# Two of eight value taps as ScalarE products that GpSimd adds, in the wavelet-attention and binary-conv kernel

## The reference

```python
x = x + L0(group_norm(x))      # attention over channels
x = x + L1(group_norm(x))      # two binary 3x3 convolutions with batch norms
```

```python
kv = depthwise3x3(einsum('oc,bchw->bohw', qkv_w, x));  k, v = split(kv)
q  = inverse_dwt(depthwise3x3(dwt(x)))                 # a wavelet transform there and back
attn = softmax(normalised(q) @ normalised(k).T * temperature)   # 16x16 a head and image
out  = proj_w @ (attn @ v)
```

## Time and profile before

| | us |
|---|---|
| median of three runs | 1533.03 |
| lowest, highest | 1522.18, 1548.53 |
| the profiled execution | 1536.24 |
| its span | 1534.7 |
| its stretch from 224 to 1006 us, nearly all of `block_grams` | 782 |

### The profile page before, as it was taken

The page is one execution under the profiler, slowest core; times in us unless marked ns, Lnnn a source line. Parts: engine busy times, 40 slices in busy tenths (PEclk is TensorE's granted clock), DMA queues, the critical chain, the costliest instruction groups (busy, mean ns, idle before and its releaser), DMA issues. The chain is left out here.

```text
span 1534.7 us, 35991 instructions
## 1 busy us (share of the span) xinstructions
PE 1222.0 (80%) x12628; PEld 975.4 (64%) x12628; DVE 1140.8 (74%) x1567; ACT 790.9 (52%) x1382; POOL 492.9 (32%) x268
## 2 busy tenths in 40 slices
PE   1797837789898889898988889863699999799910
PEld 0454537779898889897988889851355555455500
DVE  7626938999989899998999999924776673253384
ACT  0475745556555656565655657511134425666473
POOL 1486912344453292542613736311100000000000
PEclk9999958798989899898998999975899999899965
DMA  9975763434343443334343434116877622000059
GB/s 330 365 293 219 305 151 81 116 82 116 83 119 82 121 116 93 107 95 116 90 117 83 119 92 117 60 34 238 288 278 246 204 70 103 1 0 1 0 230 401
DMA packets 147827, 221.12 MB, mean 144 GB/s; under 512 B 115528, under 2 KB 116692, under 8 KB 144096
## 3 DMA queue, kind: packets, MB, share of 16 engines
q1 hardware_dynamic: 137888, 166.41, 34.8%
q0 software_dynamic: 5184, 33.03, 5.8%
q10 hardware_dynamic: 4608, 19.67, 3.2%
HBM read 131.84 MB, written 87.20 MB: 143 GB/s over the span
## 5 line engine op out<-in xcount | busy, mean ns | idle before, releaser
L844 DVE SCALAR_TENSOR_TENSOR b_vacc<-b_vin,b_vtaps,b_vacc 128x1152 f32<-128x1152 f32 x256 | 430.7, 1682 | 0.0
L1566 PE MATMUL b_conv_bank<-b_sign,wsign 128*128 (+1 forms) x1728 | 296.7, 328 | 10.3 <-ACT b_sign L1346 7.7
L803 ACT CAST b_feat<-b_bank 96x400 f16<-96x400 f32 x255 | 125.0, 490 | 290.3 <-PE b_bank L887 290.2
L885 PE MATMUL b_bank<-b_yh,b_tmh 96*96 96x200 f16 x768 | 205.4, 267 | 71.1 <-DVE b_yl L850 57.9
L1566 PEld LDWEIGHTS b_conv_bank<-b_sign,wsign 128*128 128x128 bf16 x1728 | 168.6, 98 | 141.5 <-issue 29.6
L885 PE MATMUL b_bank<-b_tkh,b_kt 96*96 96x100 f16 x1536 | 248.2, 222 | 3.5 <-DVE b_tml L866 3.3
L886 PE MATMUL b_bank<-b_tkl,b_kt 96*96 96x100 f16 x1536 | 247.1, 222 | 0.0
L887 PE MATMUL b_bank<-b_tkh,b_kt 96*96 96x100 f16 x1536 | 246.4, 221 | 0.0
L645 POOL TENSOR_TENSOR b_xl<-b_xraw,b_xh 96x1536 f16<-96x1536 f32 x32 | 119.5, 3735 | 387.1 <-ACT b_xh L768 387.1
L885 PEld LDWEIGHTS b_bank<-b_tkh,b_kt 96*96 96x96 f16 x1536 | 211.6, 138 | 5.2 <-DVE b_tml L866 3.5
L887 PEld LDWEIGHTS b_bank<-b_tkh,b_kt 96*96 96x96 f16 x1536 | 210.9, 137 | 0.0
(11 more groups left out here) (205 smaller groups left out, 2533.5 us busy)
## 6 DMA issues: line engine op xcount, KB each, us to landing
b_vin<-value_projection_scratch SPq DMA_DIRECT2D x32, 686.0 KB, 5.2
value_projection_scratch<-b_vout ACTq DMA_DIRECT2D x24, 784.0 KB, 3.3
keys_scratch<-b_khl SPq DMA_DIRECT2D x24, 784.0 KB, 3.3
b_kt<-keys_scratch SPq DMA_DIRECT2D x128, 147.0 KB, 2.9
b_xraw<-in_x SPq DMA_DIRECT2D x128, 144.0 KB, 4.9
values_scratch<-b_vacc SPq DMA_DIRECT2D x32, 576.0 KB, 3.2
b_values<-values_scratch SPq DMA_DIRECT2D x48, 384.0 KB, 3.7
out<-xs SPq DMA_DIRECT2D x25, 576.0 KB, 7.1
```

The lines of the kernel that those rows point to most:

```text
L803: nc.scalar.copy(*target(n, 0, k)).then_inc(s_hi, 1)
L844: nc.vector.scalar_tensor_tensor(acc, src, vtaps[:, t:t + 1], acc, ALU.mult, ALU.add).then_inc(s_tap, 1)
L885: nc.tensor.matmul(out, w_hi, m_hi, start=first, stop=False)
L1566: ins = nc.tensor.matmul(cbank[k % NBK][:, 0:CH].rearrange("p (r c) -> p r c", c=W), p["wsign"][nth // NIMG][:, t * C:(t + 1) * C], padded ...
```

## The change

Of the eight taps on VectorE six remain, behind the low parts of jobs 2, 5, 8, 11, 14 and 17. The taps 7 and 8 become products that ScalarE writes into a new tile `vprod`, before its copies of jobs 6 and 15, and two additions on GpSimd (`add_products`), which wait for the sixth tap. They stand in each group's GpSimd queue behind `low_x`, and so ahead of `null_parts`. SyncE's store of the slab waits for the second addition; ScalarE's product m of a group waits for addition m of the group before.

Room: `xraw` has one buffer, and the load of the rows of group i + 2 waits for `low_x(i + 1)`; `gout` holds one half of the gram, is stored in parts (behind the second and the fourth group of a head), and the copy of the second half waits for the first one's store; `eprod` is halved and `null_parts` goes through it one side at a time, with twelve operations and more waits between them.

```diff
-        xraw = sb("b2_xraw", [H, 2, CI * W])
+        xraw = sb("b2_xraw", [H, CI * W])
...
-        eprod = sb("b2_eprod", [W, 4, 2, NIMG * HD * 2])
+        eprod = sb("b2_eprod", [W, 2, 2, NIMG * HD * 2])
...
+        vprod = sb("b2_vprod", [C, 2, SLAB * W])
-        gout = sb("b2_gout", [2 * HD * RUN, NIMG, RUN, 4 * HD])
+        gout = sb("b2_gout", [2 * HD * RUN, 2, RUN, 4 * HD])
...
-        TAPS = [1, 3, 6, 8, 11, 13, 16, 18]
+        TAPS = [2, 5, 8, 11, 14, 17]
+        PRODUCTS = [6, 15]
...
+        STORE_AT = [1, 3, 3]
...
+            load_rows(0)
             for i in range(2):
-                load_rows(xraw, d["x_rows"], s_xin, i, i)
                 load_keys(i, i)
             for i in range(2):
                 load_slab(i * SLAB * WP, i)
+            sp.wait_ge(s_xl, 1)
+            load_rows(1)
...
                 if ahead:
-                    sp.wait_ge(s_xl, i + 1)
+                    sp.wait_ge(s_xl, i + 2)
                     sp.sem_inc(s_carry, 1)
-                    load_rows(xraw, d["x_rows"], s_xin, i + 2, slot)
+                    load_rows(i + 2)
...
-                sp.wait_ge(s_tap, i * 8 + 8)
+                sp.wait_ge(s_vfin, i * 2 + 4)
                 sp.sem_inc(s_carry, 1)
                 sp.dma_start(d["values"][:, ds(i * (SLAB * W), SLAB * W)], vacc[:, slot, :]).then_inc(s_vst[slot], 16)
...
 (null_parts, behind the four b_edge sums)
                 for side in range(2):
+                    at_step = 4 + side * 3
                     for j in range(2):
                         nc.gpsimd.tensor_tensor(
-                            eprod[:, side * 2 + j, :, :].rearrange("p s (n r) -> p s n r", r=2),
+                            eprod[:, j, :, :].rearrange("p s (n r) -> p s n r", r=2),
                             edge[:, side, :, :, :, :].rearrange("p s b e r -> p s (b e) r"),
                             null_cols[:, side * 2 + j, :, :].unsqueeze(2).broadcast_to([W, 2, NIMG * HD, 2]),
                             ALU.mult).then_inc(s_estep, 1)
...
+                    pool.wait_ge(s_estep, base + (at_step + 2))
+                    pool.sem_inc(s_carry, 1)
+                    nc.gpsimd.tensor_tensor(esum, esum, eprod[:, :, 1, :], ALU.add).then_inc(s_estep, 1)
+                    pool.wait_ge(s_estep, base + (at_step + 3))
+                    pool.sem_inc(s_carry, 1)
+                    ends = esum.rearrange("p a (n r) -> p a n r", r=2)
+                    nc.gpsimd.tensor_tensor(enull[:, side * 2:side * 2 + 2, :], ends[:, :, :, 0], ends[:, :, :, 1],
+                                            ALU.add).then_inc(s_edge, 1)
+                    pool.wait_ge(s_edge, head * 2 + (side + 1))
+                    pool.sem_inc(s_carry, 1)
+
+            def add_products(i, slot):
+
+                for m in range(2):
+                    if m == 0:
+                        pool.wait_ge(s_tap, i * 6 + 6)
+                    else:
+                        pool.wait_ge(s_vfin, i * 2 + (m + 2))
+                    pool.sem_inc(s_carry, 1)
+                    pool.wait_ge(s_prod, i * 2 + (m + 1))
+                    pool.sem_inc(s_carry, 1)
+                    nc.gpsimd.tensor_tensor(vacc[:, slot, :], vacc[:, slot, :], vprod[:, m, :], ALU.add).then_inc(s_vfin, 1)
 
             def body(k, i, how):
                 if how != LAST:
...
                     low_x(i + 1, (k + 1) % 2)
+                add_products(i, k % 2)
...
+            def product(k, i, m):
+
+                slot, t = k % 2, 7 + m
+                act.wait_ge(s_vfin, i * 2 + (m + 1))
+                nc.scalar.activation(vprod[:, m, :].rearrange("p (r c) -> p r c", c=W),
+                                     vin[:, slot, :].rearrange("p (r c) -> p r c", c=WP)[:, t // 3:t // 3 + SLAB, t % 3:t % 3 + W],
+                                     ACT.Copy, scale=vtaps[:, t:t + 1]).then_inc(s_prod, 1)
+
             def body(k, i, pairs, how, gram=None):
 
                 for n, (kind, c, old) in enumerate(jobs):
+                    if n in PRODUCTS:
+                        product(k, i, PRODUCTS.index(n))
```

More of the change, by code:

```diff
@@ L479, in block_grams @@
         s_z = sem("b2_pads_zeroed")
-        s_xin = [sem(f"b2_x_rows_in{k}") for k in range(2)]
+        s_xin = sem("b2_x_rows_in")
         s_kin = [sem(f"b2_key_rows_in{k}") for k in range(2)]
@@ L620, in _ @@
                 for k in range(PAIR):
-                    if k == GPH:
-                        store_gram(hh * 2)
                     body(PEEL + k, hh * PAIR + (PEEL + k), hh + (PEEL + k + 2) // (NG // NIMG), True)
-                store_gram(hh * 2 + 1)
+                    for e in range(GPARTS):
+                        if k % GPH == STORE_AT[e]:
+                            store_gram(hh * 2 + k // GPH, e)
             for i in range(NG - GPH, NG):
                 body(i, i, (i + 2) // (NG // NIMG), i + 2 < NG)
-            store_gram(HEADS - 2)
-            store_gram(HEADS - 1)
+                for e in range(GPARTS):
+                    if i % GPH == STORE_AT[e]:
+                        store_gram(HEADS - 2, e)
+            for e in range(GPARTS):
+                store_gram(HEADS - 1, e)
+            sp.wait_ge(s_xin, NG * LOAD)
             for slot in range(2):
-                sp.wait_ge(s_xin[slot], NG // 2 * LOAD)
                 sp.wait_ge(s_kin[slot], NG // 2 * LOAD)
@@ L700, in _ @@
             pool.wait_ge(s_c, 7 * 16)
+            pool.sem_inc(s_vfin, 2)
             spread_taps(0, 0)
@@ L767, in high_x @@
                 act.wait_ge(s_xn, i + 1)
-                nc.scalar.copy(xh[0][:, slot, :, :, :].rearrange("h b c w -> h (b c w)"), xraw[:, slot, :]).then_inc(s_xh, 1)
+                nc.scalar.copy(xh[0][:, slot, :, :, :].rearrange("h b c w -> h (b c w)"), xraw[:]).then_inc(s_xh, 1)
             def first_tap(k, loads):
@@ L779, in copy_gram @@
             def copy_gram(head, e):
-                if e == 0:
-                    act.wait_ge(s_gst, head * GST + GST)
+                if e < GPARTS - 1:
+                    act.wait_ge(s_gst, head * GST + (GST + e * RUN * 16))
                 act.wait_ge(s_gram, head * GPARTS + (e + 1 + GPARTS))
                 if e < GPARTS - 1:
-                    ins = nc.scalar.copy(gout[:, 2 * e:2 * e + 2, :, :].rearrange("p b r f -> p b f r"),
+                    ins = nc.scalar.copy(gout[:].rearrange("p b r f -> p b f r"),
                                          gbank[:].rearrange("p (b f r) -> p b f r", b=2, r=RUN))
@@ L807, in _ @@
             act.sem_inc(s_gout, 1)
-            normalise(0, 0, 1)
+            normalise(0)
             high_x(0, 0)
@@ L938, in gram_null @@
             def gram_null(head):
-                pe.wait_ge(s_edge, head + 1)
+                pe.wait_ge(s_edge, head * 2 + 2)
                 pe.wait_ge(s_gout, head * GPARTS + GPARTS)
```

46 lines of the change are left out of this document (22 added, 24 removed).

## The result

The change made the kernel **slower**: 1582.89 us median of four executions (1572.46 to 1587.10), against 1537.79 for the kernel before on the same chip; ratio 1.0298, 95% interval 1.0246 to 1.0350. The same file, run again later beside other kernels, gave 1567.20, ratio 1.0162 (1.0117 to 1.0207). One of the repeat's four executions, 1583.93 us, was in a slower state and is not in the ratio. The two intervals do not overlap, so the loss is between 1 and 3.5 per cent; both lie above 1.

The account below looks back on a forecast made before the run. VectorE was taken to hold 22.9 us of work in each 24.4 us group. Gains of 8.4 in groups 0 to 3 and 3.5 over seven heads, together 12 off 1536.2, gave 1524; median 3 lower, 1521; range 1455 to 1580.

Parts of the forecast that it names:

- Taps and products: In each group two taps leave VectorE, -2.7 us; ScalarE gets two products of 1.25 us, hidden.
- The adds hold 2.0 us of taps in every group: GpSimd's two additions, 2.9 us each, run back to back and hold VectorE's second tap of the next group about 2.0 us.
- Once per head, GpSimd is late, L = 10: Additions delay `null_parts`, then `low_x`, the single-buffer x load and `normalise`; VectorE gets job 4 late: 10 us lost a head.
- The single x buffer costs nothing in other groups: Outside the late group, the x load just fits: 7 to 8 us remain for the 6.4 needed.
- The group of 22.3: A group without `null_parts`: 10.1 + 6 x 1.33 + 2.2 + 2.0 = 22.3 us, against 24.4, with no idle time.
- the second rival: At job 0, TensorE drops to half clock; VectorE idles 3.5, group 23.8, a head loses 12: 1583 us; chance 0.20.

Follow-up runs that it names:

- no_adds: The changed kernel without the two GpSimd additions; the products are made and never added: 1505.90 us, ratio 0.9804 to the kernel before.
- null_first: The changed kernel with `null_parts` ahead of the additions of their group in GpSimd's queue: 1517.78 us, ratio 0.9862 to the kernel before.
- room_only: The changed kernel's buffers and split gram copy, all eight taps on VectorE, no products, no additions: 1563.93 us, ratio 1.0176 to the kernel before.
- room_two_x: room_only with the second x buffer back: 1549.19 us, ratio 1.0080 to the kernel before.
- six_taps: The kernel before with six taps at the changed places, the last two left out, nothing added: 1509.68 us, ratio 0.9854.
- six_apart: taps_apart with two taps left out, six behind jobs 1, 2, 4, 6, 8, 18: 1458.86 us, ratio 0.9464 to the kernel before.
- taps_apart: The kernel before with its eight taps moved, none from job 9 to 16, where `low_x` runs: 1486.30 us, ratio 0.9692.
- the fillers: Throw-away matmuls ahead of job 0 in the changed kernel, six_taps and an eight-tap kernel with taps placed away from `low_x`: ratios 1.0230, 0.9707, 0.9706.

## Why the prediction was wrong

By its own steps:

- **Taps and products**: right. 192 taps; products 1.265 us (1.25); GpSimd's adds 2.61 to 2.63 (2.9 taken, bounds 2.3 and 2.9).
- **The adds hold 2.0 us of taps in every group**: wrong, it is 0.2 (8 taps and 7.1 us in the whole stage). The adds fall into VectorE's idle time, which I had struck out.
- **Once per head, GpSimd is late, L = 10**: right in place, chain and size: 11.3 us by no_adds, and null_first takes most of it away.
- **The single x buffer costs nothing in other groups**: right as put (`normalise` waits in seven groups only); but with eight taps and no adds it costs 25 us of the stage (room_only against room_two_x), in the groups behind `null_parts` that were slow already, and with six taps and no adds nothing in those groups (22.1 us in no_adds and in six_taps). In the changed kernel it is part of the late head's loss, not on top of it (the long group is within 1.1 us of the forecast).
- **The group of 22.3**, "the idle 1.5 goes because TensorE then has no stretch as empty as 613 to 618 and should keep its full clock": **this step failed**. The stretch stayed (437 to 443: 1.9 us of work in 6), the clock fell behind it (443 to 450: 0.50), and the idle time, put at nothing, grew from 1.5 to 2.7 us a group with the relief alone, and to 4.6 with everything. In the three ordinary groups of a head it is 3.1, and the sum of such a group is 10.1 + 8.0 + 1.9 held + 3.1 idle = 23.1 us (23.3 in the mean of the six whole heads), not 10.1 + 8.0 + 2.2 + 2.0 = 22.3. Groups 0 to 3 take 27.1 in the mean, 5.7 of it idle.

In numbers of the stage: forecast 781.7 - 12 = 770, measured 812.5. Groups 0 to 3 took 108.5 us where 8.4 less than before (101.9) was forecast, 93.5: 15 of the 42.5. The heads took 103.3 where 99.2 was forecast: three ordinary groups 1.0 over 22.3, and the long one 33.4 for 32.3; about 4 us, seven times, is the other 27. Against the profiled execution's 1584.05 us the forecast was 1524: of these 60, 42.5 lie in the stage, 15 ahead of it (the later first tap, which unchanged work shows as well) and 2 behind.

The place and the sizes are those of the second rival, "the clock falls oftener", which I had given 0.20; that the half clock is what costs the time is not shown. It put an idle time of 3.5 behind job 0 at half clock and a group of 23.8, and 12 us lost a head; measured are waits of 1.03 and 2.43 behind ScalarE's copies of jobs 0 and 1 (3.46 together), groups of 23.3, and 11.3. It gave 1583; the median is 1582.9, part of which is luck, since 15 us of that profile are the first tap's and the repeat has 1567.20. What made me prefer the other: I read the empty stretch as an echo of one held tap, and held it for cured because VectorE would have slack. But the tap that stands behind job 11 meets `low_x` in the changed order too (4.16 us at 460.29), and removing two other taps doesn't shorten it (31 taps meet a `low_x` in both kernels, for 69 us before and 72 after).

What the runs show in its place: taps taken off VectorE turn in good part into waiting, whether or not a tap is held. With the hold at `low_x` in place (six_taps), 84 us of work less bring 44.8 us of stage, and the idle time goes from 1.5 to 2.7 us a group. Without the hold (six_apart against taps_apart), 73 us bring 18, and it goes from 1.7 to 3.4. So the held tap is not what makes the idle time: taps_apart removes it and VectorE idles (721.4 - 667.1) / 32 = 1.7 us a group, no less than before, though the waits for `b_feat` fall from 49.7 to 37.6 us and the clock rises from 0.90 to 0.94; its gain of 60.3 us goes with the 66 us that VectorE is busy less, the holding itself. The prediction also had TensorE at 18.2 us a group at full clock and called it no bound; in six_apart, at a mean granted clock of 0.95, it is busy 20.3 of 22.0.

What stays open is how the idle time of six_taps (2.7 us a group) splits between the half clock and the plain order of the jobs, in which VectorE and TensorE wait for each other by turns: with the fillers the clock rose each time, and the time fell once, rose once and once did neither. Groups 0 to 3 gained nothing from the relief (102.7 us in six_taps, 101.9 before): VectorE idles 5.2 us in each of them, where it was 3.2, and is held 2.2, where it was 1.7. Why it is more there than in the heads was not looked into.

## What to carry to other kernels

Before moving work off a busy engine, ask how much of its busy time is held time: here 71 of 733 us were taps waiting for another engine's read, and placing the same eight taps elsewhere gained 4.3% (0.9500 to 0.9636) where moving two of them to other engines, as the change did, lost. Count a relief only as far as the idle time beside it doesn't grow: of 84 us of work taken away 45 reached the stage, of 73 another time 18. On a queue that runs in order, put the work that somebody waits for ahead of the work that nobody does: one such move was worth 47 of the 63 us that two additions a group had cost.

## What had not been expected of the hardware

- A 128x1152 f32 addition on GpSimd takes 2.61 us undisturbed, 2.27 ns an element, less than the 2.56 worked out from the smaller additions of the earlier trace rows; beside a tap up to 4.05.
- A load of x rows lands 2.7 to 2.8 us after its issue in the median of every kernel here with one x buffer, and 4.7 to 4.9 in every one with two (before: the earlier trace rows; room_two_x: 4.7). It was not looked into why. In the late head shown `normalise` starts 6.1 us after `low_x` ends, where 6.4 was forecast.
- With matmuls thrown in, the mean granted clock of the stage went up by 0.04 to 0.07 in three kernels, and the time fell by 1.5% in one, rose by 1.4% in another and did not visibly move in the third.
- The same instructions reach the first tap at 225 to 227 us in some executions and at 236 to 240 in others, in kernels that are alike up to there (but for the first tap's place, behind job 1 or 2); one file did both, 239.6 and 227.0.
